# Eight of sixteen query heads left unnormalised, their scale moved into the exponentials, and a new order of the pieces

## The reference, cut to what matters

```python
q, k, v = split(shift_tokens(x) @ Wqkv)        # 16 heads of 64
q = q / norm(q) * qs
k = k / norm(k) * ksc
q = q * cos * scale + rotate_half(q) * sin * scale
k = k * cos / scale + rotate_half(k) * sin / scale
sim = einsum('bhwie,bhwje->bhwij', bq, bk2) * 8.0     # own window and the one before
attn = softmax(where(mask, -max, sim))
x = einsum(attn, bv2) @ Wo + x
x = (a * gelu(gate)) @ W2 + b2 + x             # a, gate from layernorm(shift_tokens(x)) @ W1
```

## Time and profile before

| | us |
|---|---|
| median of 3 runs | 4875.62 (4875.0 to 4887.95) |
| the profiled execution | 4875.73 |
| its span | 4874.4 |
| the last stage in it, from about 1400 | about 3470 |
| PE busy | 4219.5 (87%) |
| DVE busy | 3887.6 (80%) |
| POOL busy | 3717.0 (76%) |
| ACT busy | 3235.4 (66%) |

### The profile page before, as it was taken

The page is one execution under the profiler, slowest core; times in us unless marked ns, Lnnn a source line. Parts: engine busy times, 40 slices in busy tenths (PEclk is TensorE's granted clock), DMA queues, the critical chain, the costliest instruction groups (busy, mean ns, idle before and its releaser), DMA issues.

```text
span 4874.4 us, 139104 instructions
## 1 busy us (share of the span) xinstructions
PE 4219.5 (87%) x57664; PEld 3041.7 (62%) x57664; DVE 3887.6 (80%) x6471; ACT 3235.4 (66%) x5034; POOL 3717.0 (76%) x2624
## 2 busy tenths in 40 slices
PE   7886566658868999999999999999999999999997
PEld 5664455546635666666666666666666666666665
DVE  4665999935557888888888888888888888888994
ACT  4664888844435677677776767666776676767775
POOL 1112888833358998899998989889998898988993
PEclk9998787889988999999999999999999999999999
DMA  2000000000001222222222222222222222222222
GB/s 60 2 2 1 1 1 1 1 26 2 2 1 42 52 51 59 57 53 54 54 58 55 56 52 51 64 55 57 50 60 59 55 53 51 60 53 56 51 57 55
DMA packets 120832, 198.72 MB, mean 41 GB/s; under 512 B 66896, under 2 KB 78224, under 8 KB 120080
## 3 DMA queue, kind: packets, MB, share of 16 engines
q1 hardware_dynamic: 120208, 189.82, 15.9%
HBM read 24.12 MB, written 2.10 MB: 5 GB/s over the span
## 4 chain that ended last, share of the span: by engine, by line
PE 54%; ACT 13%; DVE 11%; issue 8%; POOL 6%; DMA 6%; SPq 1%; DVEq 0%; ACTq 0%; POOLq 0%
PE ps L1306 8%; PE ps L1250 8%; PE ps L1251 7%; DMA arena<-arena 6%; PE ps L1259 5%; DVE arena L1489 3%; PE ps L1347 3%; PE ps L1358 2%; PE ps L1297 2%; PE ps L1341 2%; PE ps L1298 2%; ACT L1393 2%; PE ps L1278 2%; DVE arena L1482 2%; DVE arena L598 2%
## 5 line engine op out<-in xcount | busy, mean ns | idle before, releaser
L1582 POOL TENSOR_TENSOR arena<-arena 128x1024 f32<-128x1024 f32 x384 | 909.1, 2368 | 237.2 <-DVE arena L1482 236.9
L1577 POOL TENSOR_TENSOR arena<-arena 128x32 f32<-128x32 f32 x192 | 1045.4, 5445 | 0.1
L1481 DVE TENSOR_TENSOR arena<-ps,arena 128x1024 f32<-128x1024 f32 x384 | 470.2, 1224 | 314.9 <-ACT arena L1376 314.9
L1376 ACT ACTIVATE arena<-ps 128x1024 f32<-128x1024 f32 x384 | 393.0, 1024 | 375.1 <-PE ps L1251 370.5
L1600 POOL TENSOR_TENSOR arena<-arena 128x1536 f32<-128x1536 f32 x192 | 529.1, 2756 | 111.9 <-DVE arena L1515 111.9
L208 POOL TENSOR_SCALAR arena<-arena 128x2 f32<-128x2 f32 x256 | 72.7, 284 | 628.1 <-DVE arena L202 617.0
L1306 PE MATMUL ps<-arena 96*64 96x64 f32 x12288 | 424.4, 228 | 73.1 <-DMA arena<-arena 68.6
L1482 DVE TENSOR_TENSOR arena<-ps,arena 128x1024 f32<-128x1024 f32 x384 | 466.0, 1213 | 0.0
L1306 PEld LDWEIGHTS ps<-arena 96*64 96x64 f32 x12288 | 397.6, 140 | 105.0 <-issue 97.2
L1489 DVE TENSOR_REDUCE arena<-arena 128x32 f32<-128x2048 f32 x192 | 436.8, 2275 | 0.0
L1250 PE MATMUL ps<-arena 128*128 128x512 f32 x768 | 433.1, 646 | 0.9 <-ACT arena L1425 0.9
(11 more groups left out here) (251 smaller groups left out, 10039.7 us busy)
## 6 DMA issues: line engine op xcount, KB each, us to landing
arena<-arena SPq DMA_DIRECT2D x192, 384.0 KB, 4.4
arena<-arena SPq DMA_DIRECT2D x192, 256.0 KB, 3.7
arena<-arena SPq DMA_DIRECT2D x192, 128.0 KB, 2.3
arena<-in_dWqkv SPq DMA_DIRECT2D x18, 512.0 KB, 3.6
arena<-arena SPq DMA_DIRECT2D x96, 64.0 KB
arena<-arena SPq DMA_DIRECT2D x96, 63.5 KB
arena<-in_dWo SPq DMA_DIRECT2D x6, 512.0 KB, 4.9
arena<-in_x SPq DMA_DIRECT2D x4, 512.0 KB, 7.4
```

The costliest lines, as they stand in the source:

```text
L1376: act.activation(SQ[:, 1024 * g:1024 * g + 1024], ps(f"q{g}", n), ACT.Square).then_inc(*sq[g].up())
L1481: dve.tensor_tensor(o1, p.rearrange("p (h e) -> p h e", h=16), bc(cs, 1, 16), ALU.mult)
L1577: pool.tensor_tensor(ss[:, 0:32], ss[:, 32:64], mhalf32, ALU.pow).then_inc(*S.rs.up())
L1582: pool.tensor_tensor(a1[:, half], a1[:, half], T2[:, half], ALU.add).then_inc(*radd[g].up())
```

## The change

Three edits, all in `phase_d`. First, the queries of heads 0 to 7 are no longer multiplied by their inverse length: nrm0 works on columns 512 to 1023 alone. Second, ex0, the exponentials of those eight heads, becomes eight activations of 96 elements, each with the inverse length of its head as the activation's scale (a value per partition, read through a pointer). Before them ACT waits for rs of the tile, and rs waits for ex0 of three tiles earlier, since it reuses that buffer of lengths. Third, all numbers of TILE, BATCH, LAYER and EDGE are new, so every engine's order changes.

```diff
-    TILE = {"radd0": 0, "radd1": 114, "rs": 635, "ro0": 924, "ro1": 1055, "ssum": 1085, "halo": 1229, "nrm0": 1313,
-            "q0": 1338, "q1": 1606, "sq0": 1810, "sq1": 1922, "nrm1": 2759, "t0": 3300, "t1": 3445, "mx0": 3478,
-            "mx1": 3743, "qT": 3797, "s0": 3881, "kT": 3888, "s1": 4013, "pn": 4899, "ex0": 5254, "ex1": 5460,
-            "sum": 5842, "v": 6623, "p0": 6684, "p1": 6859, "vn": 7022, "vd": 7122, "xxa": 7210, "o": 7233,
-            "pT0": 7309, "pT1": 7427, "oT": 7658, "wo": 7722}
-    BATCH = {"sh": 189, "xs": 558, "fd": 10497, "fst": 12624, "frs": 13777, "fn": 16105, "ft": 16779, "fgm": 16933,
-             "fg": 16960, "fzT": 17348, "fge": 17533, "fa": 17592, "xxf": 17640, "fo": 17970}
-    LAYER = {"lqk": 32650, "lv": 37700, "lwo": 38900, "lw1": 47700, "lw2": 48200, "tab": 16000}
-    EDGE = {"e0": 19570, "e1": 20630, "e2": 22580, "e3": 22630, "out": 25000}
+    TILE = {"ro0": 40, "ro1": 135, "q0": 195, "radd0": 197, "q1": 200, "rs": 239, "ssum": 340, "radd1": 535,
+            "nrm0": 626, "sq0": 650, "sq1": 660, "halo": 947, "nrm1": 1662, "t0": 1857, "qT": 2036, "t1": 2174,
+            "kT": 2655, "mx0": 2769, "mx1": 2801, "s0": 3006, "s1": 3103, "ex0": 3460, "pn": 3732, "ex1": 3861,
+            "sum": 4019, "v": 5293, "p0": 5370, "vn": 5780, "pT0": 5801, "vd": 5880, "p1": 6032, "o": 6259,
+            "pT1": 6361, "xxa": 6461, "wo": 6727, "oT": 6779}
+    BATCH = {"sh": 0, "xs": 343, "fd": 9064, "fst": 11433, "frs": 11543, "fn": 14419, "ft": 14806, "fzT": 14864,
+             "fg": 15220, "fgm": 15414, "fa": 15445, "fge": 15761, "xxf": 15858, "fo": 16122}
+    LAYER = {"tab": 16000, "lqk": 31250, "lv": 36373, "lwo": 37877, "lw1": 45545, "lw2": 46322}
+    EDGE = {"e0": 17788, "e1": 18848, "e2": 20798, "e3": 20848, "out": 23218}
...
                 act.wait_ge(*sub[g].at(n + 1))
-                act.activation(P, P, ACT.Exp).then_inc(*ex[g].up())
+                if g == 0:
+                    act.wait_ge(*S.rs.at(n + 1))
+                    for x in range(8):
+                        h = 2 * (x % 4) + x // 4
+                        i = act.activation(P[:, x, :], P[:, x, :], ACT.Exp, scale=SS[n % 3][:, h:h + 1])
+                    i.then_inc(*S.ex0.up())
+                else:
+                    act.activation(P, P, ACT.Exp).then_inc(*S.ex1.up())
...
                     pool.wait_ge(*S.nrm_k.at(n - 2))
+                    pool.wait_ge(*S.ex0.at(n - 2))
                 pool.wait_ge(*S.ssum.at(n + 1))
...
-                a3 = a1[:, 0:1024].rearrange("p (h e) -> p h e", h=16)
-                pool.tensor_tensor(a3, a3, bc(ss[:, 0:16], 2, 64), ALU.mult).then_inc(*S.nrm_q.up())
+                a3 = a1[:, 512:1024].rearrange("p (h e) -> p h e", h=8)
+                pool.tensor_tensor(a3, a3, bc(ss[:, 8:16], 2, 64), ALU.mult).then_inc(*S.nrm_q.up())
```

## The result

The changed kernel takes 4638.16 us, median of 4 runs (4630.38 to 4640.9), against 4881.78 us for the one before in the same sessions: ratio 0.950, interval 0.9475 to 0.952. Forecast were 4752 us and a range that ended at 4712. The direction and the main mechanism, that three waits of TensorE go, held; the gain is 5.0% where 2.5% was forecast.

What follows compares the result with a forecast made beforehand. TensorE was taken to set the pace: idle falling from 2.0 to 0.6 us a pair gave 1.4 x 88.3 pairs = 124 us, with fill and drain at 0, so 4875.7 - 124 = 4752 us; range 4712 to 4838.

Steps and rivals of the forecast that it cites:

- three waits of TensorE: Steady part: TensorE idles only before fo, fg and o, 1.0, 0.5 and 0.5 us a pair, 2.0 us at best to gain.
- ex0 at 2.2 us: ScalarE: eight exponentials at 0.27 us each take 2.2 us, +1.4 us per tile, bounds 2.0 and 3.5 us.
- nrm0 at 0.95: GpSimd: nrm0 on 512 elements takes 0.95 us instead of 1.90, so GpSimd loses 1.9 us a pair.
- the wait of GpSimd before the even rs: GpSimd waits 2 to 3 us for ssum before each even rs.
- no wait for the copies of V: TensorE's o: 10.6 us from vn to o where about 6.5 are needed, so the wait of 0.5 us is gone.
- the term for scatter: TensorE's idle after: today's irregular wait, 40.2/85.5 = 0.47 us a pair, taken for scatter on margins of 0 to 0.6.
- the 0.15 for q0: TensorE: q0[1] wants mx0's slot just as it is freed, nothing spare, some 0.15 us lost.
- TensorE's work as a constant: Steady part: TensorE's work of 33.1 us a pair was kept for the new order; only idle time was to fall.
- fill and drain at 0, within 10: The stage's fill and drain, idle 62 of 250 and 33 of 124 us: change 0, within 10 us.
- GpSimd with nothing spare: GpSimd's round ends at 43.8, where the next radd0 is due; with a full nrm0 it would run 1.9 us behind.
- All of it: Rival, chance 0.17: margins hold, idle 0.2 us a pair, drain shorter, gain 164 us: 4712 us.
- the arithmetic costs nothing: ScalarE: ex0's extra 1.4 us are hidden with 0.3 spare, covered by ScalarE's own idle time.

## Why the prediction was right in kind and wrong in size

**Held.** TensorE bounds the kernel, three waits were all that could be had, and the new order takes all three away. ex0 at 2.2 us (2.23, so 1.4 more than before, as by the row, and not 0.65), hidden; nrm0 at 0.95 (1.04); the wait of GpSimd before the even rs of 2.3 us (2.26) and before the odd of 0.5 (0.49); no wait for the copies of V. Laying the order out by hand with the durations of the rows gave these within 0.1 us.

**Failed: the term for scatter.** "For scatter on margins of 0 to 0.6 I take today's irregular wait", 0.47 us a pair, against 0.13 us measured for everything, the 0.15 for q0 included. The irregular wait of before had one cause, a DMA with too little room, and that cause was gone by my own list. Taking it for a general scatter counted it a second time: 43 us (167 measured, 124 forecast).

**Failed: TensorE's work as a constant.** The sum took 33.1 us a pair for before and after. It is 32.61 in the new order, with either arithmetic, and 33.13 to 33.15 in four of the six kernels in the old order (33.5 and 34.8 in the two with the longest waits, whose clock fell at times). That is 48.5 us over the stage. Of the 0.53 us a pair, 0.10 to 0.15 go with the waits, as above, and t1's place alone is worth about 0.1. From start to start, in the means between 2500 and 3300, q0 and q1 of both tiles take 7.14 us instead of 7.44, wo 3.77 instead of 3.87, o 4.12 instead of 4.22 and fg 1.39 instead of 1.46, and v 3.83 instead of 3.70; but of the neighbours only t1 was moved by itself, so why each of them changed is argued and not shown. The rows to see it were read: q takes 1.92 us between two small pieces, and the new order puts q1 right behind q0.

**Failed: fill and drain at 0, within 10.** The waits there fell by 28 us (18 and 10), 22 if the 6 us that the lists of waits give too much are taken off here. In the fill o no longer waits for the copies of V (24.6 us before, none after), and the waits of t for nrm0 and nrm1 fell from 34.1 to 31.3 in all. By the kernel with the order alone, whose fill waits are 47 us, most of it is the order's too. The three terms, 43 + 48.5 + 22 = 113.5 us, less 3 for the stages ahead, leave 110 of the 111 us by which the profiled execution stayed below 4752.

**Failed: GpSimd with nothing spare.** "With a full nrm0 it would run 1.9 us behind; this is what the halved one buys." My list had GpSimd waiting 2.3 and 0.5 us for ssum inside the same round, and a wait is room: lateness eats it first. The order alone is 33 us slower than the whole change, not 150. The halving of nrm0 and ex0's new form together do pay, for less; the two were not tried one by one in the new order.

**The rivals.** "All of it", at 4712, was the nearest, and even it had only the waits. That the arithmetic costs nothing holds in the new order alone: in the old one the arithmetic cost 284 us, and 286 came back once pT0 no longer stood behind ex0's 1.4 us.

## What to carry to other kernels

An order of pieces can be judged from rows: put each engine's queue on one clock, and ask at every take of a buffer how much is spare. Name the cause of a wait before it is carried over into the sum as scatter, and count an engine's own waits inside a round as its slack. Where TensorE is the bound, count also what stands beside what: the same matmuls took 1.6% less in another order, about a quarter of that by the ends that waits leave; and a small delay ahead of a buffer's release can be free in one order and 6% in another (284 of 4881 us).

## What the runs showed of the hardware

**An operation of VectorE with two SBUF inputs, already running, holds GpSimd's rs up.** rs, 32 values to a power, takes 5.43 to 5.46 us in all 192 cases before. In the kernels after, with the order alone and in the runs with radd1 and nrm1 moved, it takes 6.2 to 6.5 us in each of the 424 cases where nrm1, which reads two SBUF operands in 1.22 us, is running when rs starts, and 5.43 to 5.47 in all others. An operation of VectorE with one operand in PSUM does not do it: with fgm (L1537) running for 0.6 to 1.2 us more, rs keeps its 5.44. Nor does nrm1 when it starts after rs, and then it is hardly held up itself: 1.28 us in the kernel after, where it starts 0.05 us behind rs. The Trainium skill, "GPSIMD Engine Reference", Specifications, states such contention of GpSimd with VectorE operations that have two SBUF inputs; the runs agree, by 0.8 to 1.0 us, where VectorE was first. In the kernel with the order alone it cost GpSimd (5.95 - 5.45) x 2 = 1.0 us a pair, on an engine that was nearly full there.

**The clock fell behind waits of 2.4 us that recur in every pair.** With fo waiting 1.0 us a pair the granted clock was 1.00 in the steady part; with 2.4 us, and 1.0 in the other half, it was 0.95. Around the wait shown above it fell to 0.50 and 0.55 for 7 us, and fo took 2.90 us instead of 1.5; behind two other such waits, at 3072 and 3110, fo took 1.70 and 1.97.
